# Cross-attention with a top-k mask and a mixture of experts on one core: the front of the work re-ordered over VectorE, ScalarE and GpSimd

## The chip, the core and the metric

The kernel runs on one core of one Trainium2 chip. The metric is the device time of one execution in microseconds (us). The kernel before takes 130.39 us (median of three runs, 130.18 to 130.52).

## What is computed

The input is four batches of 256 tokens with 256 features (x) and 256 context tokens with 64 features (ctx). Two stages follow each other, each with a residual:

```
# stage 1, per batch
Q = ctx @ Wq.T ; K = ctx @ Wk.T
sim = Q K^T / (sqrt(16) * 4)                     # 256 x 256
threshold = 76th largest of each row of sim      # int(0.3 * 256)
A = sigmoid(sim) * (sim >= threshold) ; A = (A + A^T) / 2
g = sigmoid(gamma_raw)
x1 = x + (1 - g) * layernorm(x) + g * A
# stage 2, all tokens
xn = layernorm(x1)
probs = softmax(xn @ gate_w) ; two best of 8 experts, their scores normalised, times alpha
h_e = gelu(xn @ fc1_w[e] + fc1_b[e]) ; y_e = h_e @ fc2_w[e] + fc2_b[e]
out = x1 + sum over e of combine[:, e] * y_e
```

## The kernel before

**Numbers.** The products of stage 2 are made in a reduced-precision 32-bit type, each operand split in a high and a low part, w = w_hi + w_lo, and three products are summed: hi*hi, hi*lo, lo*hi. So every expert's weights (128x1024 per partition layout, fc1 and fc2 together) need a high part (a cast, `weight_hi`) and a low part. For experts 0 and 1 GpSimd subtracts (`weight_lo(e, j)`, L675, j = 0 for fc1 and 1 for fc2). For experts 2 to 7 ScalarE writes -w_hi into w_lo (`weight_neg`, L559), and a DMA issued by GpSimd adds w to it in place (`weight_rest`, L671, below called the low-part DMA). PE waits for that DMA before `up(e)` of batch 0.

**Steps.** 32 steps s = 8b + e, batch b and expert e. On PE `up(s)` makes the hidden layer (12 products) and `down(s)` the output (12 products), down two steps behind up. Per step ScalarE does the gelu and the high part of the hidden layer (`hidden_hi`), GpSimd its low part (`hidden_lo`, h_lo, L698), and VectorE multiplies with the combine weight and adds (`add_expert`, acc, L1061). `up(s)` waits for the gelu of step s-2, `down(s)` for `add_expert(s-2)`.

**Batch b+1 beside the steps of batch b.** The mask and both layer norms of batch b+1 are spread over the steps of batch b. Batch 0 has no steps to hide behind: everything before `up(0)` is the front. What a front is, for batch 0, in the order of VectorE's program (L1073 to L1108): copy sim, mean and spread give a guess of the threshold; two sign counts on ScalarE (`signs_of`, `signs_again_of`) improve it (`middle_guess`, `better_guess`); `count_above` counts the values above the guess; `flag_few` and `flag_missed` flag rows for which the guess is too far off, PE sums the flags (`sum_missed`); `drop_above` removes the values above the guess, and two rounds of `take_eight`/`drop_eight` (MAX8 and MATCH_REPLACE8) find the 16 next; `choose` picks the threshold among them; `mask` multiplies; `add_masked` adds half of A to the base (x times mul1 plus add1, from `ln1_affine` and `base`). PE transposes the masked tile (`transpose_masked`, L374), VectorE's `residual` adds the transpose and makes the moments of the second layer norm, GpSimd its power -1/2 (`rstd`), VectorE `normalise` (xn, L971), PE transposes xn (`transpose_xn`), ScalarE and VectorE copy its high and low part (`xt_hi_of`, `xt_lo_of`), and `up(0)` starts.

**Order.** Each engine runs its own program in a hand-written order, and all waits are semaphores. On PE, after the similarities of the four batches (`similarities`, L357, with `sum_missed(0)` between those of batches 1 and 2), come `transpose_masked(0)`, 18 dummy products (`keep_warm(WARM_BEFORE_XN)`, L355), `transpose_xn(0)`, three more, then the steps. Loads are issued by the sync engine in one order (L307 to L317). On GpSimd the order is a list (L701 to L739), so a step that waits holds all behind it: there the high parts of experts 0 to 2, `rstd`, `base(0)`, the low parts, the low-part DMAs, and in the steps `hidden_lo`, `rstd`, the DMAs and `add_masked`. ScalarE has the high parts of experts 3 to 7 (L555).

## Time and profile before

| | |
|---|---|
| median of three runs | 130.39 us (130.18 to 130.52) |
| the profiled execution | 130.1 us, its span 128.3 us |
| PE busy | 119.2 us, 93% of the span |
| VectorE (DVE) busy | 96.2 us, 75% |
| ScalarE (ACT) busy | 87.6 us, 68% |
| GpSimd (POOL) busy | 65.0 us, 51% |
| read from HBM, written | 8.81 MB, 1.05 MB |

Engines in the rows: PE is TensorE, PEld its weight load, DVE VectorE, ACT ScalarE, POOL GpSimd, SP the sync engine. A row of the timeline has start, duration, engine, line, operation, out<-in, shapes, count, and in brackets the idle time before it with what ended it. Busy PE is not PE at its peak: the dummy products count as busy. Times are us from the start of the span.

### The profile page before, as it was taken

The numbers are of one execution on the slowest core, as the hardware profiler recorded it, in microseconds if no ns is written. First come the engines' busy times: TensorE is split into PE (matmuls) and PEld (weight loads), VectorE is DVE, ScalarE is ACT, GpSimd is POOL, SyncE is SP. The second block draws the span as 40 slices with busy tenths as digits, with TensorE's granted clock in tenths as the row PEclk, the third lists the DMA queues.
The fourth block names the chain that finished last, engine by engine and source line by source line (L and its number), as shares of the span: only waits on it lengthen the run. The fifth ranks groups of instructions, "written<-read, shape, count | busy, mean of one in ns | idle before, by whom it ended". The sixth has DMA issues, their size and how long they took to land.

```text
span 128.3 us, 2763 instructions
## 1 busy us (share of the span) xinstructions
PE 119.2 (93%) x904; PEld 108.6 (85%) x904; DVE 96.2 (75%) x399; ACT 87.6 (68%) x212; POOL 65.0 (51%) x66
## 2 busy tenths in 40 slices
PE   6796989899969999999999999999999999999990
PEld 3443656699949999999899999998999999999990
DVE  0068989886987898999979999999787337823481
ACT  3178999899999979454897784729646544555510
POOL 2039668638647944643097456512972545444400
PEclk9999999999999999999999999999999999999999
DMA  2999999952996000002000000200000002000002
GB/s 66 198 390 415 405 321 174 192 101 29 181 169 119 5 0 3 0 5 82 3 0 0 3 8 0 81 1 8 0 0 0 5 0 82 0 5 0 3 0 82
DMA packets 3380, 10.05 MB, mean 78 GB/s; under 512 B 396, under 2 KB 868, under 8 KB 3364
## 3 DMA queue, kind: packets, MB, share of 16 engines
q1 hardware_dynamic: 2500, 6.71, 14.7%
q0 software_dynamic: 864, 3.15, 14.3%
q8 instruction: 7, 0.11, 0.3%
q14 instruction: 9, 0.07, 0.2%
HBM read 8.81 MB, written 1.05 MB: 77 GB/s over the span
## 4 chain that ended last, share of the span: by engine, by line
PE 41%; DVE 36%; ACT 13%; issue 6%; POOL 1%; DVEq 0%; POOLq 0%; ACTq 0%
PE p_y L477 17%; PE p_h L455 16%; DVE acc L1061 8%; ACT h_act L579 3%; ACT w_lo L564 2%; ACT w_hi L557 2%; DVE top L886 2%; DVE above L842 2%; DVE stats L745 2%; ACT h_hi L587 2%; PE p_y L355 2%; DVE left L891 1%; DVE picked L1018 1%; ACT act_waste L543 1%; DVE best_f L1004 1%
## 5 line engine op out<-in xcount | busy, mean ns | idle before, releaser
L698 POOL TENSOR_TENSOR h_lo<-h_act,h_hi 128x512 fp32r<-128x512 f32 x31 | 40.2, 1300 | 45.4 <-ACT h_hi L587 32.6
L579 ACT ACTIVATE h_act<-p_h,small_sb 128x256 f32<-128x256 f32 x64 | 26.6, 467 | 19.4 <-PE p_h L455 19.3
L455 PE MATMUL p_h<-xt_hi,w_hi 128*128 128x256 f32 x128 | 32.9, 280 | 1.1 <-ACT h_act L579 1.0
L455 PE MATMUL p_h<-xt_hi,w_lo 128*128 128x256 f32 x128 | 32.6, 278 | 0.0
L1061 DVE SCALAR_TENSOR_TENSOR acc<-p_y,comb,acc 128x256 f32<-128x256 f32 x55 | 24.0, 475 | 11.0 <-PE p_y L477 10.2
L477 PE MATMUL p_y<-w_hi,h_hi 128*128 128x256 f32 x126 | 26.0, 288 | 1.0 <-DVE acc L1061 1.0
L455 PEld LDWEIGHTS p_h<-xt_hi,w_hi 128*128 128x128 f32 x128 | 24.1, 188 | 1.6 <-issue 1.5
L455 PE MATMUL p_h<-xt_lo,w_hi 128*128 128x256 f32 x128 | 25.3, 279 | 0.0
L477 PE MATMUL p_y<-w_lo,h_hi 128*128 128x256 f32 x126 | 24.9, 279 | 0.0
L477 PE MATMUL p_y<-w_hi,h_lo 128*128 128x256 f32 x126 | 24.9, 279 | 0.0
L455 PEld LDWEIGHTS p_h<-xt_hi,w_lo 128*128 128x128 f32 x128 | 24.1, 188 | 0.0
L587 ACT ACTIVATE h_hi<-h_act 128x512 fp32r<-128x512 f32 x32 | 20.2, 630 | 0.9
L477 PEld LDWEIGHTS p_y<-w_hi,h_hi 128*128 128x128 f32 x126 | 19.1, 189 | 1.7 <-issue 1.5
L455 PEld LDWEIGHTS p_h<-xt_lo,w_hi 128*128 128x128 f32 x128 | 19.5, 188 | 0.1
L477 PEld LDWEIGHTS p_y<-w_lo,h_hi 128*128 128x128 f32 x126 | 19.3, 189 | 0.0
L477 PEld LDWEIGHTS p_y<-w_hi,h_lo 128*128 128x128 f32 x126 | 19.2, 188 | 0.0
L355 PE MATMUL p_y<-warm 128*128 128x256 bf16 x30 | 6.5, 395 | 1.2 <-DVE warm L1073 1.2
L669 POOL CAST w_hi<-w_sb 128x1024 fp32r<-128x1024 f32 x3 | 3.1, 1035 | 7.0 <-DMA w_sb<-w 7.0
L886 DVE MAX8 top<-left 128x8 f32<-128x256 f32 x16 | 5.9, 410 | 0.8 <-DVE left L891 0.4
L355 PEld LDWEIGHTS p_y<-warm 128*128 128x128 bf16 x30 | 4.1, 140 | 2.8 <-DVE warm L1073 1.2
L564 ACT ACTIVATE w_lo<-w_hi 128x1024 fp32r<-128x1024 f32 x6 | 6.3, 1047 | 0.1
L593 ACT ACTIVATE x_sb<-x_sb,add,mul 128x256 f32<-128x256 f32 x6 | 3.3, 591 | 4.1 <-DVE add L791 4.1
(141 smaller groups left out, 191.1 us busy)
## 6 DMA issues: line engine op xcount, KB each, us to landing
w_sb<-w SPq DMA_DIRECT2D x8, 512.0 KB, 8.3
w_lo<-w POOLq DMA_DIRECT2D x6, 512.0 KB, 5.6
x_sb<-x SPq DMA_DIRECT2D x1, 768.0 KB, 8.5
out<-acc SPq DMA_DIRECT2D x3, 256.0 KB, 2.5
x_sb<-x SPq DMA_DIRECT2D x1, 256.0 KB, 4.4
out<-acc SPq DMA_DIRECT2D x2, 128.0 KB, 2.0
attn_sb<-attn SPq DMA_DIRECT2D x1, 192.0 KB, 5.1
small_sb<-small SPq DMA_DIRECT2D x1, 97.5 KB, 4.7
```

What stands on the lines that cost most here:

```text
L355: nc.tensor.matmul(p_y[1][:, 0:N], warm[:, 0:P], warm[:], start=True, stop=True)
L455: last = nc.tensor.matmul(dst, w_[:, e, 0, k, c * P:(c + 1) * P], v[:, b % 2, k, :], start=n == 0, stop=n == len(trio) - 1)
L477: last = nc.tensor.matmul(dst, v[:, s % (LAG + 1), k, t * P:(t + 1) * P], w_[:, e, 1, k, :], start=n == 0, stop=n == len(trio) - 1)
L557: nc.scalar.activation(w_hi[:, e], w_sb[:, e], ACT.Copy).then_inc(w_hi_ready, 1)
L564: nc.scalar.activation(w_lo[:, e], w_hi[:, e], ACT.Copy, scale=-1.0).then_inc(w_neg_ready, 1)
L579: last = nc.scalar.activation(h_act[:, s % 2, c], tiled(p_h[s % 2])[:, c, :], ACT.Gelu, bias=b1_sb[:, e, c:c + 1])
L587: nc.scalar.activation(h_hi[:, s % (LAG + 1)], h_act[:, s % 2], ACT.Copy).then_inc(h_hi_ready, 1)
L593: last = nc.scalar.activation(x_sb[:, b, t], x_sb[:, b, t], ACT.Identity, scale=mul1[:, b, t:t + 1], bias=add1[:, b, t:t + 1])
L669: nc.gpsimd.tensor_copy(w_hi[:, e], w_sb[:, e]).then_inc(w_hi_early, 1)
L698: nc.gpsimd.tensor_tensor(h_lo[:, s % (LAG + 1)], h_act[:, s % 2], h_hi[:, s % (LAG + 1)], ALU.subtract).then_inc(h_lo_ready, 1)
L886: step_of_tile(nc.vector.max(top[:, t, 8 * r:8 * r + 8], left[:, t]))
L1061: last = nc.vector.scalar_tensor_tensor(acc[:, b % 2, t], tiled(y_bank(s, t))[:, t, :], comb[:, b, t, 0, e:e + 1], so_far, ALU.mult, ALU.add)
```

## The change

- **Loads.** The small tensor (gamma, alpha, gate weights, biases, identity) is issued second instead of fourth.
- **Gamma.** ScalarE makes tanh of gamma, and the high part of the gate weights, right after its first copy; VectorE's `gamma_terms` stands at the very front instead of before `drop_above(0)`.
- **Batch 0's affine.** `ln1_affine(0)`, four instructions of 128x1, moves from VectorE to GpSimd.
- **Threshold of batch 0.** The two tiles' guess and count instructions are interleaved; `flag_few` and `flag_missed` become one instruction of 128x2 each instead of two of 128x1 (in every batch), and `flag_missed` stands after both tiles of `drop_above`.
- **Moments of batch 1.** `ln1(1)` moves on VectorE from between `add_masked(0)` and `residual(0)` to step 1, and GpSimd's `rstd` for it from step 0 to step 1.
- **Casts.** The high parts of experts 5, 6, 7 move from ScalarE to GpSimd (before step 0, in step 0 and in step 2); ScalarE keeps 3 and 4. GpSimd's list before the steps is re-ordered, and the low-part DMA of expert 4 moves from before step 0 into it, the DMAs of experts 5 to 7 one step back each.
- **ScalarE's order.** `sim_copy(1)` and `spread_of(1)` come before the negated weights of experts 2 and 3, `base(1)` one step later (step 3), the high part of b2 in step 5 instead of 3; VectorE's `b2_parts_of` in step 6 instead of 4.

PE's program keeps its order; only the count that `sum_missed` waits for changes.

```diff
--- before.py
+++ after.py
@@ -27,7 +27,9 @@
 REPLACED = -3.0e38
 ROUNDS = 2
 DAMPINGS = (0.8, 0.5)
-POOL_HI = 3
+POOL_HI = (0, 1, 2, 5, 6, 7)
+ACT_HI = (3, 4)
+POOL_HI_AT = {0: 6, 2: 7}
 WARM_FIRST = 9
 WARM_BEFORE_XN = 18
 B2_AFTER = 4
@@ -305,9 +307,9 @@
         def _(sp):
             first = 2 * D + N
             sp.dma_start(attn_sb[:, 0:first], attn[:, 0:first]).then_inc(attn_in, 16)
+            sp.dma_start(small_sb[:], small).then_inc(small_in, 16)
             sp.dma_start(x_sb[:, 0], x[:, 0:TILES]).then_inc(x_in[0], 16)
             sp.dma_start(attn_sb[:, first:], attn[:, first:]).then_inc(ctx_in, 16)
-            sp.dma_start(small_sb[:], small).then_inc(small_in, 16)
             sp.dma_start(w_sb[:, 0], w[:, 0]).then_inc(w_in[0], 16)
             for e in range(1, EXPERTS):
                 sp.dma_start(w_sb[:, e], w[:, e]).then_inc(w_in[e], 16)
@@ -341,7 +343,7 @@
 
             def sum_missed(b):
 
-                pe.wait_ge(missed_ready, (b + 1) * TILES)
+                pe.wait_ge(missed_ready, b + 1)
                 if b == 0:
                     pe.wait_ge(u_copied, 1)
                     pe.wait_ge(const_set, 2)
@@ -557,10 +559,10 @@
                 nc.scalar.activation(w_hi[:, e], w_sb[:, e], ACT.Copy).then_inc(w_hi_ready, 1)
 
             def weight_neg(e):
-                if e < POOL_HI:
-                    act.wait_ge(w_hi_early, e + 1)
+                if e in POOL_HI:
+                    act.wait_ge(w_hi_early, POOL_HI.index(e) + 1)
                 else:
-                    act.wait_ge(w_hi_ready, e - POOL_HI + 1)
+                    act.wait_ge(w_hi_ready, ACT_HI.index(e) + 1)
                 nc.scalar.activation(w_lo[:, e], w_hi[:, e], ACT.Copy, scale=-1.0).then_inc(w_neg_ready, 1)
 
             def xt_hi_of(b):
@@ -602,28 +604,27 @@
             act.wait_ge(m_ready, 1)
             nc.scalar.activation(m_sb[:], p_g[0:D, 0:D], ACT.Copy).then_inc(m_copied, 1)
             u_copy(0)
+            act.wait_ge(small_in, 16)
+            nc.scalar.activation(gam[:, 0:1], gamma_sb, ACT.Tanh, scale=0.5).then_inc(gam_th, 1)
+            nc.scalar.activation(gate_parts[:, :, 0], gate_sb, ACT.Copy).then_inc(gate_hi_ready, 1)
             sim_copy(0)
             spread_of(0)
             signs_of(0)
             signs_again_of(0)
-            act.wait_ge(small_in, 16)
-            nc.scalar.activation(gam[:, 0:1], gamma_sb, ACT.Tanh, scale=0.5).then_inc(gam_th, 1)
             for b in range(1, BATCHES):
                 u_copy(b)
             sigmoid(0)
+            weight_hi(3)
+            sim_copy(1)
+            spread_of(1)
             weight_neg(2)
-            weight_hi(3)
             weight_neg(3)
-            for b in range(1, BATCHES):
+            for b in range(2, BATCHES):
                 sim_copy(b)
-            nc.scalar.activation(gate_parts[:, :, 0], gate_sb, ACT.Copy).then_inc(gate_hi_ready, 1)
-            spread_of(1)
-            weight_hi(4)
-            weight_neg(4)
             signs_of(1)
             xt_hi_of(0)
             signs_again_of(1)
-            weight_hi(5)
+            weight_hi(4)
             for s in range(STEPS):
                 b, e = divmod(s, EXPERTS)
                 more = b + 1 < BATCHES
@@ -638,16 +639,19 @@
 
                     act.wait_ge(gap_ready, b + 1)
                     nc.scalar.activation(gap_th[:], gap[:], ACT.Tanh, scale=0.5).then_inc(gap_th_ready, 1)
-                if s < 3:
-                    weight_neg(5 + s)
                 if s < 2:
-                    weight_hi(6 + s)
-                if s == 3:
+                    weight_neg(4 + s)
+                if s in (1, 3):
+                    weight_neg(6 + s // 2)
+                if s == 5:
                     act.wait_ge(b2_in, 16)
                     nc.scalar.activation(b2_hi[:], b2_sb[:], ACT.Copy).then_inc(b2_hi_ready, 1)
                 if e == 2 and more:
                     sigmoid(b + 1)
-                    base(b + 1)
+                    if b:
+                        base(b + 1)
+                if s == 3:
+                    base(1)
                 if e == 5:
                     comb_hi_of(b)
                 if e == 4 and b + 2 < BATCHES:
@@ -685,6 +689,18 @@
                                                    add1[:, b, t:t + 1], ALU.mult, ALU.add)
                 last.then_inc(base_ready, 1)
 
+            def ln1_affine(b):
+
+                pool.wait_ge(gam_ready, 1)
+                pool.wait_ge(ln1_agg, (b + 1) * TILES)
+                pool.wait_ge(ln1_rstd, b + 1)
+                for t in range(TILES):
+                    nc.gpsimd.tensor_scalar(mul1[:, b, t:t + 1], rstd1[:, b, t:t + 1], gam[:, 2:3], ones[:], ALU.mult,
+                                            ALU.add)
+                    last = nc.gpsimd.tensor_scalar(add1[:, b, t:t + 1], mv1[:, b, t, 0:1], gam[:, 3:4],
+                                                   rstd1[:, b, t:t + 1], ALU.mult, ALU.mult)
+                last.then_inc(ln1_mul, 1)
+
             def add_masked(b):
 
                 pool.wait_ge(masked, (b + 1) * TILES)
@@ -706,30 +722,32 @@
             weight_hi(0)
             rstd(veps1, rstd1, 0, ln1_veps, ln1_rstd)
             weight_lo(0, 0)
-            weight_hi(1)
-            weight_hi(2)
+            ln1_affine(0)
             base(0)
-            weight_lo(1, 0)
-            weight_rest(2)
             pool.wait_ge(gate_hi_ready, 1)
             nc.gpsimd.tensor_tensor(gate_parts[:, :, 1], gate_sb, gate_parts[:, :, 0], ALU.subtract).then_inc(
                 gate_lo_ready, 1)
+            weight_hi(1)
+            weight_hi(2)
+            weight_lo(1, 0)
+            weight_rest(2)
+            rstd(veps2, rstd2, 0, ln2_veps, ln2_rstd)
+            pool.wait_ge(xn_ready, TILES)
+            weight_lo(0, 1)
             weight_rest(3)
-            pool.wait_ge(masked, TILES)
-            weight_lo(0, 1)
-            rstd(veps2, rstd2, 0, ln2_veps, ln2_rstd)
-            weight_rest(4)
-            pool.wait_ge(xn_ready, TILES)
             weight_lo(1, 1)
+            weight_hi(5)
             for s in range(STEPS):
                 b, e = divmod(s, EXPERTS)
                 more = b + 1 < BATCHES
                 if s < STEPS - 1:
                     hidden_lo(s)
-                if s == 0:
+                if s == 1:
                     rstd(veps1, rstd1, 1, ln1_veps, ln1_rstd)
-                if s < 3:
-                    weight_rest(5 + s)
+                if s < 4:
+                    weight_rest(4 + s)
+                if s in POOL_HI_AT:
+                    weight_hi(POOL_HI_AT[s])
                 if more and b and e == 0:
                     rstd(veps1, rstd1, b + 1, ln1_veps, ln1_rstd)
                 if more and e == 3:
@@ -827,16 +845,22 @@
                 nc.vector.tensor_scalar(neg_middle[:, b, t:t + 1], off_first[:, t:t + 1], -PER_COUNTS[0] / 2,
                                         neg_guess[:, b, t:t + 1], ALU.mult, ALU.add).then_inc(middle_ready, 1)
 
-            def better_guess(b, t):
+            def offset_again(b, t):
 
                 dve.wait_ge(signs_again_ready, b * TILES + t + 1)
                 nc.vector.tensor_scalar(off[:, t:t + 1], signs_again[:, b, t:t + 1], N - 2 * MIDDLE,
                                         spread[:, b, t:t + 1], ALU.add, ALU.mult).then_inc(off_ready, 1)
+
+            def second_guess(b, t):
                 dve.wait_ge(off_ready, b * TILES + t + 1)
                 nc.vector.tensor_scalar(guess[:, t:t + 1], off[:, t:t + 1], PER_COUNTS[1] / 2,
                                         neg_middle[:, b, t:t + 1], ALU.mult,
                                         ALU.subtract).then_inc(better_ready, 1)
 
+            def better_guess(b, t):
+                offset_again(b, t)
+                second_guess(b, t)
+
             def count_above(b, t):
                 dve.wait_ge(better_ready, b * TILES + t + 1)
                 nc.vector.tensor_scalar(above[:, t], sim[:, b, t], guess[:, t:t + 1], None, ALU.is_ge, ALU.add,
@@ -844,19 +868,16 @@
 
             def flag_few(b):
 
-                for t in range(TILES):
-                    dve.wait_ge(counted, b * TILES + t + 1)
-                    nc.vector.tensor_scalar(few[:, t:t + 1], count[:, t:t + 1], TOP_K - WINDOW, None,
-                                            ALU.is_lt).then_inc(few_ready, 1)
+                dve.wait_ge(counted, (b + 1) * TILES)
+                nc.vector.tensor_scalar(few[:], count[:], TOP_K - WINDOW, None, ALU.is_lt).then_inc(few_ready, 1)
 
             def flag_missed(b):
 
                 if b:
                     dve.wait_ge(missed_sum, b)
-                for t in range(TILES):
-                    dve.wait_ge(few_ready, b * TILES + t + 1)
-                    nc.vector.tensor_scalar(missed[:, t:t + 1], count[:, t:t + 1], TOP_K, few[:, t:t + 1],
-                                            ALU.is_ge, ALU.add).then_inc(missed_ready, 1)
+                dve.wait_ge(few_ready, b + 1)
+                nc.vector.scalar_tensor_tensor(missed[:], count[:], TOP_K, few[:], ALU.is_ge,
+                                               ALU.add).then_inc(missed_ready, 1)
 
             steps = [0]
 
@@ -876,9 +897,11 @@
                 for t in range(TILES):
                     dve.wait_ge(counted, b * TILES + t + 1)
                     if t == TILES - 1:
-                        flag_missed(b)
+                        if b == 0:
+                            flag_few(b)
                     step_of_tile(nc.vector.scalar_tensor_tensor(left[:, t], above[:, t], REPLACED, sim_of_tile(b, t),
                                                                 ALU.mult, ALU.add))
+                flag_missed(b)
 
             def take_eight(r):
                 for t in range(TILES):
@@ -1071,6 +1094,7 @@
 
 
             nc.vector.memset(warm[:], 1.0).then_inc(warm_set, 1)
+            gamma_terms()
             for t in range(1, TILES):
                 sim_copy(t)
             for t in range(TILES):
@@ -1084,13 +1108,13 @@
                 ln1_variance(0, t)
             for t in range(TILES):
                 middle_guess(0, t)
-            for t in range(TILES):
-                better_guess(0, t)
-                count_above(0, t)
-            flag_few(0)
-            gamma_terms()
+            offset_again(0, 0)
+            second_guess(0, 0)
+            offset_again(0, 1)
+            count_above(0, 0)
+            second_guess(0, 1)
+            count_above(0, 1)
             drop_above(0)
-            ln1_affine(0)
             take_eight(0)
             know_missed(0)
             drop_eight(0)
@@ -1099,7 +1123,6 @@
             choose(0)
             mask(0)
             add_masked(0)
-            ln1(1)
             residual(0)
             guesses(1)
             normalise(0)
@@ -1123,6 +1146,7 @@
                 if more and e == 1:
                     take_eight(0)
                 if s == 1:
+                    ln1(1)
                     combine(0)
                 if more and e == 1:
                     drop_eight(0)
@@ -1137,7 +1161,7 @@
                     take_eight(1)
                     choose(nxt)
                     mask(nxt)
-                if s == 4:
+                if s == 6:
                     b2_parts_of()
                 if more and e == 5:
                     residual(nxt)
```

## Rows read from the trace of the kernel before

**Rows 1.** The page: busy time and instructions of the engines.

```profile
PE 119.2 (93%) x904; PEld 108.6 (85%) x904; DVE 96.2 (75%) x399; ACT 87.6 (68%) x212; POOL 65.0 (51%) x66
```

**Rows 2.** The chain that ended last, in order of time: start, us, what.

```profile
18.93 0.66 DVE stats L745 x2
...
19.92 0.75 DVE x L957 x2
...
22.57 0.43 DVE xn L971
...
38.60 1.60 PE p_h L455 x12
```

**Rows 3.** The timeline of PE in the front.

```profile
15.57 1.91 PE L339 MATMUL p_y<-attn_sb,u_sb 64*128 64x256 f32 x4
18.02 1.08 PE L379 MATMUL p_a<-small_sb,half 128*128 128x128 f32 x4 [0.54 <-DVE half L941]
18.90 3.89 PE L355 MATMUL p_y<-warm 128*128 128x256 bf16 x18
23.14 0.31 PE L391 MATMUL p_x<-small_sb,xn 128*128 128x128 f32 x1 [0.35 <-DVE xn L971]
```

**Rows 4.** Who waited for whom: PE, from 24 to 64 us (total, times, longest).

```profile
PE p_h L455 <- ACT h_act L579: 1.0, 1, 1.0
```

**Rows 5.** The timeline of VectorE in the front.

```profile
13.77 0.21 DVE L789 TENSOR_SCALAR mul<-rstd,gam 128x1 f32<-128x1 f32 x1
14.38 0.74 DVE L886 MAX8 top<-left 128x8 f32<-128x256 f32 x2
17.06 0.22 DVE L897 SCALAR_TENSOR_TENSOR chosen<-small_sb,count,top 128x16 f32<-128x16 f32 x1
17.39 0.48 DVE L941 SCALAR_TENSOR_TENSOR half<-p_s,threshold,half 128x256 f32<-128x256 f32 x1
```

**Rows 6.** The timeline of GpSimd up to 28 us.

```profile
0.75 0.10 POOL L702 MEMSET ones<- 128x1 f32 x1
9.62 0.70 POOL L665 TENSOR_TENSOR rstd<-veps,neg_half 128x2 f32<-128x2 f32 x1
11.49 2.02 POOL L669 CAST w_hi<-w_sb 128x1024 fp32r<-128x1024 f32 x2
14.57 1.09 POOL L684 TENSOR_SCALAR x_sb<-x_sb,mul,add 128x256 f32<-128x256 f32 x2 [1.07 <-DVE add L791]
15.64 1.27 POOL L677 TENSOR_TENSOR w_lo<-w_sb,w_hi 128x512 fp32r<-128x512 f32 x1
19.10 0.21 POOL L715 TENSOR_TENSOR gate_parts<-small_sb,gate_parts 128x16 fp32r<-128x16 f32 x1 [1.24 <-ACT gate_parts L619]
```

**Rows 7.** The timeline of VectorE and GpSimd, where they work at once.

```profile
39.22 1.28 POOL L698 TENSOR_TENSOR h_lo<-h_act,h_hi 128x512 fp32r<-128x512 f32 x1 [2.56 <-ACT h_hi L587]
39.46 1.31 DVE L1040 SCALAR_TENSOR_TENSOR b_parts<-b_hi,small_sb,b_sb 24x256 fp32r<-24x256 f32 x1 [0.59 <-ACT b_hi L647]
45.90 0.46 DVE L1033 SCALAR_TENSOR_TENSOR comb_parts<-comb_hi,small_sb,p_g 24x256 fp32r<-24x256 f32 x1
...
82.53 1.29 POOL L698 TENSOR_TENSOR h_lo<-h_act,h_hi 128x512 fp32r<-128x512 f32 x1 [1.44 <-ACT h_hi L587]
82.83 1.02 DVE L1004 CAST best_f<-best_at 128x4 f32<-128x4 uint32 x1
```

**Rows 8.** ScalarE's timeline from the first xt_hi copy to step 0's high part.

```profile
23.73 0.38 ACT L571 ACTIVATE xt_hi<-p_x 128x256 fp32r<-128x256 f32 x1 [0.55 <-PE p_x L391]
27.18 0.61 ACT L587 ACTIVATE h_hi<-h_act 128x512 fp32r<-128x512 f32 x1
```

**Rows 9.** DMA issues by line: KB each, median us from issue to landing.

```profile
small_sb<-small SPq DMA_DIRECT2D x1, 97.5 KB, 4.7
```

**Rows 10.** The low-part DMAs' line on GpSimd: durations of issue, spread of landing.

```profile
L673 POOL DMA_DIRECT2D w_lo<-w x6: 869/880/1002, 16.9 to 35.8; - x6
DMA to landing us min/median/max: 5.4/5.6/5.9
```

## The prediction

> **What bounds the kernel now.** I began with the page: PE is busy 93% of the span, but dummy products count as busy [rows 1], so the question is where PE's real work could start earlier or waits. The chain that ended last, read in order of time, is VectorE's in the front: moments of batch 1 at 18.93, `residual` at 19.92, xn at 22.57 [rows 2]. Next PE's timeline: the last similarities end at 17.48, the masked tiles are turned from 18.02 to 19.10, the 18 dummies run from 18.90 to 22.79, and xn is turned at 23.14 after an idle 0.35 us that VectorE's xn ended [rows 3]. Everything up to 23.14 is front, and what it loses there comes straight off the end if the steps keep their pace. In the steps up to 64 us PE's longest wait is 1.0 us for a gelu [rows 4], ahead of up(5) at 38.60 [rows 2]: a shift of the front also needs batch 0's steps to be fed earlier, not only started earlier. A measurement of this kernel tells a difference from none at about 0.3% (130.0 to 130.8 us).
>
> **VectorE's front.** Three gamma instructions and four of the affine leave; the affine took 0.61 us (13.77 to 14.38), and a gamma instruction is of the same kind and no longer [rows 5]. With the interleaved guesses and the merged flags I put MAX8 some 1.1 us earlier, at 13.2 to 13.5. Unhindered, `choose` (17.06) and `mask` (17.39) would be at 16.1 and 16.5 [rows 5]. Behind the mask `ln1(1)` goes, 0.99 us (18.93 to 19.92) [rows 2], so `residual` follows as soon as the masked tiles are turned.
>
> **What is late next: GpSimd in VectorE's way.** Beside GpSimd's h_lo from 39.22 to 40.50 VectorE's b_parts, reading two tensors of the on-chip memory, took 1.31 us and ended 0.27 after it; comb_parts, the same operation with one input from PE's banks, took 0.46. The cast best_f took 1.02 us and ended at 83.85, when GpSimd's operation ended (83.82) [rows 7]. So such an instruction stands still until the GpSimd operation that runs ends. Before, `choose` (two inputs, above_sb and top) fell at 17.06 behind GpSimd's last subtraction, 15.64 to 16.91 [rows 5, 6]; after, GpSimd has no pause there. From 11.49, when `weight_lo(0, 0)` is done, it has the affine, base(0) 1.10, the gate's low part 0.2, two casts 2.02 and `weight_lo(1, 0)` 1.25 [rows 6]. No row shows the affine on GpSimd: four instructions of 128x1, between four memsets at 0.10 (0.4 us) and four of the power instruction at 0.66 (2.6 us). I take 0.7, nearest to the 128x16 subtraction of 0.21 [rows 6]. Then `weight_lo(1, 0)` runs from about 15.5 to 16.7, `choose` waits 0.6 us until 16.7, and the mask starts at 17.0 instead of 17.39: -0.4 us. The new two-column flags may be held too, by base(0); `choose` waits anyway, so that costs nothing.
>
> By the Trainium skill, SBUF — State Buffer, section "Who interferes with whom", a VectorE instruction with two inputs in SBUF is blocked by any GpSimd instruction that reads SBUF, so by the casts as well. The rows above show it for two-input GpSimd work only; the rule adds a case to the rivals and nothing to the sum.
>
> **From mask to up(0).** Before, mask 17.39, dummies 18.90: 1.51 us between. After: dummies from 18.5, PE's similarities (end near 17.3) being done [rows 3]. The 18 dummies take 3.89 us, now to 22.4. `residual` starts near 18.7 and xn comes 2.65 later (19.92 to 22.57 before), 21.4 plus 0.4 for the instruction [rows 2]: ready ahead of the dummies, so PE, not VectorE, now sets the turn of xn, at 22.35 against 23.14: **-0.8 us**, and the idle 0.35 goes. The power instruction for it finds GpSimd free: the low-part DMA ahead of it waits for ScalarE's second negated weight until about 16.85 and issues in 1.0. The early tanh of gamma costs nothing: ScalarE idles there for PE's first similarity, and the small load, issued about 1.1 us earlier, lands by 6.0 even if it takes its old 4.7 us [rows 9].
>
> **Are the steps fed 0.8 us earlier?** ScalarE loses three casts of 1 us and has slack. GpSimd gets them. xt_hi's copy starts at 22.93, and from there to the end of step 0's h_hi it is 4.06 us as before (23.73 to 27.79), one cast between the two then and now [rows 8]: 27.0. GpSimd then: hidden_lo(0) 1.25, DMA of expert 4 0.88, cast 1.01, hidden_lo(1) 1.25, power 0.66 [rows 6, 7, 10], and issues expert 5's low-part DMA at 32.1. It lands 5.6 us later (5.4 to 5.9) [rows 10], and `up(5)` starts at 37.85; before it started at 38.60 [rows 2], after the 1.0 us wait for the gelu [rows 4]. So the gelu's wait becomes a DMA's wait, and the shift at up(5) is -0.75. Expert 4's lands at 33.8, where up(4) would be at 33.2: 0.6 us of wait, swallowed by the next. Expert 6 and 7 have over 1 us. ln1(1), 1.0 us in step 1, fills VectorE's wait for the tanh of the gap; b2_parts in step 6 meets slack of about 1 us before batch 1's xn. After up(5) the order is the old one, all shifted. `base(1)`, a step later, waits for GpSimd's cast of expert 7 on ScalarE's queue: ready near 38.5, its gelu behind it at 39.3, needed by PE at 41.3.
> One more rule: DMA: Bandwidth & Descriptors, section "Anatomy of one DMA", of the Trainium skill has such a transfer at 2.0 us plus its bytes over 436 GB/s, an estimate of 3.2 us for 512 KB, by which up(5) would wait for nothing. The trace's 5.4 to 5.9 us disagrees and decides.
>
> **Sum.** -0.8 at the turn of xn, -0.75 at up(5), and two fewer flag instructions per batch where VectorE's chain holds PE in batches 1 and 2: 0.1 us each. Together -1.0: 130.1 becomes 129.1 in the profiled execution (span 127.3). The median of before stands 0.3 above its profiled execution: **129.4 us**.
>
> **The rivals.**
> - *No hold at choose.* GpSimd's affine is as short as memsets, or the hold does not fall there. Then the mask is at 16.5, the similarities' end (17.3) and the dummies set the turn of xn near 21.75, -1.4, and up(5) follows at -1.4: 128.8 us, with -0.1 more 128.7. For it: ends of 0.4 us are near. Against: a continuous GpSimd queue.
> - *The front barely moves.* The affine costs GpSimd 2.6 us: the casts end at 17.4, and if casts hold VectorE (the skill's rule), `choose` waits for that, the mask is at 17.7 and the dummies end at 23.1: about zero, less 0.2 from the flags: 130.2 us. Or VectorE is held at several places (flags, add_masked).
> - *Slower: the low-part DMA of expert 5.* It stands behind the power instruction, which waits for ln1(1), behind best_f and MAX8 of step 1. ln1(1) ends near 30.3, the queue asks for it at 31.45, and up(5) is where it was before when the power starts at 32.2. If best_f is held by 1.0 us [rows 7] and GpSimd's queue runs 1 us late besides, with a landing of 5.9, up(5) is at 39.2: +0.6, 131.0 us. It decides from 0.75 us of lateness on.
> - *The change doesn't do what it says*: VectorE's front is freed, but the 18 dummies are kept in PE's order. This is in the sum already, as the limit of 3.89 us after the turn of the masked tiles.
>
> **Chances.** Forecast, holding 128.9 to 129.9: 0.46. No hold: 0.28. Barely moves: 0.17. Slower: 0.09. Range: 128.3 (no hold, and a landing of 5.4) to 130.4, which leaves out most of the slower case. Faster by over 0.3%: 0.46 + 0.28 + 0.05 of the third = 0.79; same 0.13; slower 0.08.
>
> **What would show it.** `choose` starts before 16.7 and lasts 0.6 us instead of 0.22, ending with `weight_lo(1, 0)`; mask 17.0. PE turns xn with no idle time named for xn, at 22.35. PE waits for DMA before up(4) and up(5), and up(5) starts near 37.85. From up(6) on all rows are the old ones shifted by 0.75 to 1.0. Wrong it is if `choose` lasts 0.22, if the turn of xn waits for VectorE, if up(5) starts without a DMA's wait or after 38.6, or if the shift at up(5) is lost by the end.

## The result, and the profile after

The changed kernel takes **138.74 us** (median of 4, 138.27 to 139.53) against 130.37 us before, a ratio of 1.065 [1.059, 1.071]: 8.4 us slower, where 1 us faster was forecast. The profiled execution is the slowest of the four: 139.53 us, span 137.7.

The page of the changed kernel: its span, busy times as in [rows 1], and the clock's row in 40 slices.

```profile
span 137.7 us, 2755 instructions
PE 122.5 (89%) x904; PEld 112.4 (82%) x904; DVE 105.3 (76%) x387; ACT 85.1 (62%) x209; POOL 69.5 (50%) x73
PEclk9999999996995599999999999999999999999999
```

VectorE, with 12 instructions fewer, is busy 9.1 us longer: its instructions last longer. The timeline of VectorE in the changed kernel says which, those of the front first (start, us; compare [rows 5]):

```profile
13.37 0.74 DVE L909 MAX8 top<-left 128x8 f32<-128x256 f32 x2
16.05 0.47 DVE L920 SCALAR_TENSOR_TENSOR chosen<-small_sb,count,top 128x16 f32<-128x16 f32 x1
16.45 1.30 DVE L920 SCALAR_TENSOR_TENSOR chosen<-small_sb,count,top 128x16 f32<-128x16 f32 x1
17.68 0.47 DVE L964 SCALAR_TENSOR_TENSOR half<-p_s,threshold,half 128x256 f32<-128x256 f32 x1
...
26.21 1.16 DVE L872 TENSOR_SCALAR few<-count 128x2 f32<-128x2 f32 x1
27.29 1.85 DVE L902 SCALAR_TENSOR_TENSOR left<-above,sim 128x256 f32<-128x256 f32 x2
29.06 2.92 DVE L879 SCALAR_TENSOR_TENSOR missed<-count,few 128x2 f32<-128x2 f32 x1
...
36.33 4.74 DVE L1046 TENSOR_TENSOR comb<-weight,small_sb 128x48 f32<-128x48 f32 x1
```

MAX8 came 1.0 us earlier, as meant. But the first `choose` lasted 0.47 and the second 1.30 us instead of 0.22 and 0.23, and behind it the mask was 0.3 us **later** than before. In the steps, a 128x2 flag lasted 2.92 us and the 128x48 product comb 4.74; the same comb takes 0.21 elsewhere. GpSimd's timeline at the same time:

```profile
14.48 2.02 POOL L673 CAST w_hi<-w_sb 128x1024 fp32r<-128x1024 f32 x2
16.46 1.25 POOL L681 TENSOR_TENSOR w_lo<-w_sb,w_hi 128x512 fp32r<-128x512 f32 x1
...
22.91 1.28 POOL L681 TENSOR_TENSOR w_lo<-w_sb,w_hi 128x512 fp32r<-128x512 f32 x1 [0.85 <-DVE xn L994]
24.13 0.89 POOL L677 DMA_DIRECT2D w_lo<-w  x1
24.77 1.60 POOL L681 TENSOR_TENSOR w_lo<-w_sb,w_hi 128x512 fp32r<-128x512 f32 x1
26.02 1.32 POOL L673 CAST w_hi<-w_sb 128x1024 fp32r<-128x1024 f32 x1
27.40 1.45 POOL L714 TENSOR_TENSOR h_lo<-h_act,h_hi 128x512 fp32r<-128x512 f32 x1
28.80 0.89 POOL L677 DMA_DIRECT2D w_lo<-w  x1
29.39 1.34 POOL L673 CAST w_hi<-w_sb 128x1024 fp32r<-128x1024 f32 x1
30.39 1.56 POOL L714 TENSOR_TENSOR h_lo<-h_act,h_hi 128x512 fp32r<-128x512 f32 x1
34.99 0.72 POOL L669 TENSOR_TENSOR rstd<-veps,neg_half 128x2 f32<-128x2 f32 x1 [3.04 <-DVE veps L775]
35.67 0.90 POOL L677 DMA_DIRECT2D w_lo<-w  x1
36.33 1.55 POOL L714 TENSOR_TENSOR h_lo<-h_act,h_hi 128x512 fp32r<-128x512 f32 x1
37.57 1.15 POOL L677 DMA_DIRECT2D w_lo<-w  x1
38.16 1.61 POOL L673 CAST w_hi<-w_sb 128x1024 fp32r<-128x1024 f32 x1
39.17 1.82 POOL L714 TENSOR_TENSOR h_lo<-h_act,h_hi 128x512 fp32r<-128x512 f32 x1
```

But for 0.06 us at 27.34, no idle time stands between the rows from 22.91 to 31.95, and none from 34.99 to 40.99. Two single VectorE instructions stood still across several GpSimd operations: the flag missed(1), 29.06 to 31.98, across the rest of a DMA issue, a cast and an h_lo, and comb, 36.33 to 41.07, across h_lo, a DMA issue, a cast and h_lo. Each ended when the run did. Others got their turn inside a run: the first `choose` ended at 16.52, with the cast (16.50), although `weight_lo(1, 0)` followed at once (16.46); few(1) ended at 27.37 with a cast (27.34); and the second `left` (1.51 of the 1.85 us are its own) ended at 29.14, when h_lo had ended (28.85) and GpSimd was issuing a DMA. PE's waits, of the whole span, say what the holds cost:

```profile
PE p_y L479 <- DVE acc L1084: 4.7, 3, 4.2
PE p_a L352 <- DVE missed L879: 2.8, 1, 2.8
```

`sum_missed(1)` stands in PE's order ahead of `down(0)`, so PE stood from 29.3 to 32.03 for the flag; `down(2)` needs `add_expert(0)`, which VectorE had behind comb. After each wait the granted clock was halved. Stretches of the changed kernel (busy PE, PEld, DVE, ACT, POOL, then PEclk, the DMA share and GB/s), and the chain:

```profile
29.00:32.00 3.00, 0.28 (x3) 0.07 (x1) 3.00 (x3) 0.63 (x1) 2.95 (x3) 0.95 0.58 75
32.00:35.00 3.00, 2.97 (x15) 2.93 (x16) 2.90 (x21) 2.25 (x4) 0.01 (x1) 0.50 0.55 107
39.00:43.50 4.50, 0.39 (x4) 0.19 (x2) 4.46 (x13) 1.88 (x4) 2.87 (x3) 0.82 1.06 199
43.50:49.00 5.50, 5.43 (x26) 5.42 (x27) 3.38 (x12) 2.61 (x9) 2.51 (x2) 0.52 0.47 83
```

```profile
36.33 4.75 DVE comb L1046
...
43.57 2.90 PE p_y L479 x12
46.47 2.49 PE p_h L457 x12
```

PE idles, then works at 0.50, the 1.2 GHz level. The sum to up(5)'s end: waits 2.8 + 4.2; down(0) 2.7 us (32.15 to 34.88) and down(2) 2.90 where a down takes 1.39 in the kernel before, up(5) 2.49 for 1.60: 3.7 more; minus 0.5 us that the front did gain, minus 1.4 for two waits of before that vanish (gelu 1.0 [rows 4], acc 0.4). That is 8.8 of the 9.4 us between the spans; the rest lies where the clock still rises.

### The profile page after: what moved, and what is told of

It is laid out like the page before. It is cut to its first block, busy times and chain, and to the rows that moved or that the text cites. A ratio compares the mean times of both kernels' runs of the same rounds, so it can differ in the third digit from the quotient of the medians.

```text
span 137.7 us, 2755 instructions
## 1 busy us (share of the span) xinstructions
PE 122.5 (89%) x904; PEld 112.4 (82%) x904; DVE 105.3 (76%) x387; ACT 85.1 (62%) x209; POOL 69.5 (50%) x73
## 3 DMA queue, kind: packets, MB, share of 16 engines
HBM read 8.81 MB, written 1.05 MB: 72 GB/s over the span
## 4 chain that ended last, share of the span: by engine, by line
PE 44%; DVE 34%; POOL 7%; issue 5%; DMA 4%; ACT 2%; SPq 1%; DVEq 1%; POOLq 0%; ACTq 0%
PE p_y L479 21%; PE p_h L457 18%; DVE acc L1084 6%; DMA w_sb<-w 4%; DVE comb L1046 4%; DVE missed L879 2%; POOL w_hi L673 2%; DVE picked L1041 2%; DVE few L872 2%; DVE left L902 2%; DVE best_f L1027 2%; DVE above L866 2%; DVE left L914 1%; DVE stats L763 1%; DVE top L909 1%
## 5 line engine op out<-in xcount | busy, mean ns | idle before, releaser
L714 POOL TENSOR_TENSOR h_lo<-h_act,h_hi 128x512 fp32r<-128x512 f32 x31 | 41.3, 1333 | 42.3 <-ACT h_hi L589 28.8
L479 PE MATMUL p_y<-w_hi,h_hi 128*128 128x256 f32 x126 | 27.1, 298 | 4.7 <-DVE acc L1084 4.7
L479 PE MATMUL p_y<-w_hi,h_lo 128*128 128x256 f32 x126 | 25.9, 288 | 0.0
L479 PE MATMUL p_y<-w_lo,h_hi 128*128 128x256 f32 x126 | 25.9, 288 | 0.0
L479 PEld LDWEIGHTS p_y<-w_hi,h_hi 128*128 128x128 f32 x126 | 20.0, 197 | 5.5 <-issue 5.3
L479 PEld LDWEIGHTS p_y<-w_lo,h_hi 128*128 128x128 f32 x126 | 20.3, 198 | 0.0
L479 PEld LDWEIGHTS p_y<-w_hi,h_lo 128*128 128x128 f32 x126 | 20.2, 197 | 0.0
L673 POOL CAST w_hi<-w_sb 128x1024 fp32r<-128x1024 f32 x6 | 7.3, 1227 | 7.4 <-DMA w_sb<-w 7.4
L669 POOL TENSOR_TENSOR rstd<-veps,neg_half 128x2 f32<-128x2 f32 x8 | 6.1, 766 | 5.5 <-DVE veps L775 3.0
L980 DVE TENSOR_TENSOR x<-x_sb,p_a 128x256 f32<-128x256 f32 x8 | 3.1, 419 | 4.3 <-PE p_a L381 2.5
```

The lines of the kernel that those rows point to most:

```text
L479: last = nc.tensor.matmul(dst, v[:, s % (LAG + 1), k, t * P:(t + 1) * P], w_[:, e, 1, k, :], start=n == 0, stop=n == len(trio) - 1)
L669: nc.gpsimd.tensor_tensor(rs[:, b, :], veps[:, b, :], neg_half[:], ALU.pow).then_inc(ready, 1)
L673: nc.gpsimd.tensor_copy(w_hi[:, e], w_sb[:, e]).then_inc(w_hi_early, 1)
L714: nc.gpsimd.tensor_tensor(h_lo[:, s % (LAG + 1)], h_act[:, s % 2], h_hi[:, s % (LAG + 1)], ALU.subtract).then_inc(h_lo_ready, 1)
```

## The experiments

Theory A, formed from the two traces: a VectorE instruction that needs what GpSimd uses gets no turn until GpSimd's queue pauses; the change made the queue unbroken. Rivals: the casts alone cost it (ScalarE or DMA order); the merged flags alone cost it; the clock costs it. Before p3 ran, a rival D was on record too: a waiting instruction gets its turn at the end of each GpSimd operation, and the next one is held anew. The kernel before, timed beside each run, took 130.44 to 130.53 us.

**x1: casts of experts 5 to 7 and their DMAs as before, the rest changed.**

```
-POOL_HI = (0, 1, 2, 5, 6, 7)    ACT_HI = (3, 4)             POOL_HI_AT = {0: 6, 2: 7}
+POOL_HI = (0, 1, 2)             ACT_HI = (3, 4, 5, 6, 7)    POOL_HI_AT = {}
```

> The changed kernel with the casts of experts 5, 6, 7 on ScalarE and the low-part DMAs where they were before; all else of the change stays. Theory A (VectorE's two-input and paired-port instructions starve while GpSimd works without a pause, and the moved casts took the pauses away): no VectorE instruction in batch 0's steps is held over 1.3 us, PE's waits of 2.8 and 4.2 us go, the clock stays at its upper level, 129.3 to 130.2 us. Rival B (the merged two-column flags are what is held, whoever casts): few and missed are still held by over 1 us, 132 us or more. Rival C (the re-ordered front itself, DMA or the small load): over 133 us.

130.68 us, 1.002 [1.001, 1.003]. So the three casts, with the places of their low-part DMAs, are 8.1 of the 8.4 us. The time is still 0.5 us above what theory A had expected. The front's gain stayed lost: the second `choose` still lasted 1.31 us, held by `weight_lo(1, 0)`, and few(1) took 1.08, the two `left` 1.85.

**x2: flags one column at a time, as before, the rest changed.**

> The changed kernel with the flags as two one-column instructions again (missed still behind both drops). Theory A: few and missed take 0.2 us each, but left in batch 0's step 0 and comb in step 1 are still held, comb until GpSimd's queue pauses (3 us or more); 133 to 138 us. Rival B: 129.5 to 130.5 us.

137.99 us, 1.061 [1.055, 1.066]. PE's wait for missed is gone, but the hold went to the next instructions. VectorE's timeline in x2:

```profile
26.34 2.78 DVE L905 SCALAR_TENSOR_TENSOR left<-above,sim 128x256 f32<-128x256 f32 x2
29.04 0.32 DVE L882 TENSOR_SCALAR missed<-count,few 128x1 f32<-128x1 f32 x2
30.42 1.59 DVE L1030 CAST best_f<-best_at 128x4 f32<-128x4 uint32 x1
34.02 2.93 DVE L1044 TENSOR_SCALAR picked<-small_sb,best_f,score 128x8 f32<-128x8 f32 x4
36.99 2.85 DVE L1047 TENSOR_TENSOR weight<-picked 128x16 f32<-128x16 f32 x1
```

The flags of one column are not held: the two few take 0.27 us at 26.15, beside GpSimd's subtraction and cast, and the two missed 0.32, beside its DMA issue. PE waited 6.6 us once for acc instead of 2.8 + 4.2. Merging the flags chose the place of the hold, not its cost. Rows with x2 or x4 add several instructions up; instruction by instruction the longest `picked` here is a single hold of 2.35 us, ended by h_lo's end (36.69), and the weight row is one instruction of 2.85.

**x3: the kernel before with only the casts and their DMAs moved to GpSimd.**

> The kernel before with nothing but the casts of experts 5, 6, 7 and the low-part DMAs moved as in the change. Theory A: one-column flags are not held, but left and one of picked, weight, comb are, 1.5 to 5 us; 132 to 137 us. Rival B: within 0.5% of the kernel before, 129.8 to 131.0 us. Rival C: the same as B.

130.95 us, 1.005 [1.003, 1.006]. The casts alone cost 0.5 us. That is the rivals' number: theory A had expected 132 to 137 us. One `picked` is held for 2.32 us (30.71 to 33.03, across a cast and an h_lo), but GpSimd's queue keeps a pause of 2.25 us ahead of the first h_lo, since `weight_lo(1, 0)` and `(0, 1)` lie in the front. PE waited 0.6 us in all for acc (1.0 in the kernel before), and 1.7 us for a low-part DMA ahead of an up. So the casts by themselves are nearly harmless, and so is the rest (x1); only together do they cost 8 us. That this is because they close the pauses is argued from the rows, not shown by x3.

**x4: the changed kernel, with two waits that make GpSimd yield.**

```
+ if s == 0: pool.wait_ge(missed_ready, 2)     # ahead of the cast of expert 6
+ if s == 2: pool.wait_ge(comb_ready, 1)       # ahead of the DMA and cast of step 2
```

> The changed kernel with two waits more on GpSimd: it lets VectorE's missed of batch 1 go before the cast of expert 6, and comb of batch 0 before the low-part DMA of expert 6 and the cast of 7. Nothing of GpSimd's work leaves. Theory A: missed and comb end with the one GpSimd instruction that runs when they come, under 1.6 us each instead of 2.9 and 4.7; PE's 4.2 us wait falls below 1.5 us; 129.5 to 132.5 us. If it is the number of casts and not their closeness: 136 us or more.

135.31 us, 1.037 [1.033, 1.040]: 3.4 of the 8.4 us back, fewer than expected: a miss. missed(1) now took 1.25, comb 0.21, but best_f (2.10) and one of the `picked` (2.12) were held and PE waited 3.7 us for acc. To yield at two places shifted the hold to the next places.

**x5: x1 with `weight_lo(0, 1)` put into GpSimd's idle time of the front.**

> The run with the casts back on ScalarE, and besides GpSimd's low part of expert 0's second half before the power instruction (where GpSimd idled from 18.8 to 21.1) instead of behind xn. Theory A: GpSimd has a pause again between its last low part and h_lo(0), so few and the two left of batch 1 are no longer held (1.08 and 1.85 us there), and the 0.7 us that the front gained reaches the end: 129.3 to 130.1 us. If the holds in step 0 were hidden anyway: 130.7 us, no change against that run.

131.77 us, 1.009 [1.006, 1.011], a miss. What it aimed at happened: left(1) took 0.76 instead of 1.85 us. But the subtraction met `add_masked`. VectorE's row, then GpSimd's:

```profile
18.74 2.44 DVE L974 TENSOR_TENSOR x_sb<-x_sb,half 128x256 f32<-128x256 f32 x2
...
18.96 1.59 POOL L683 TENSOR_TENSOR w_lo<-w_sb,w_hi 128x512 fp32r<-128x512 f32 x1
```

The pair lasted 2.44 us (0.75 before), the first of them 2.10 across the rest of a DMA issue and the whole subtraction. PE waited 2.0 us for xn, and the clock was 0.59 from 24 to 28 us.

**x6: the changed kernel with 12 dummy products ahead of `sum_missed(1)` and 18 ahead of `down(2)`.**

> The changed kernel with 12 dummy products on PE ahead of sum_missed(1) and 18 ahead of down(2), in a bank free at that time: the waits stay, the engine is busy in them. It measures what of the loss is clock: down(0), down(2) and up(5) took about 4 us more than at the upper level. If the clock's fall is a loss of its own: the granted clock stays at its upper level, 134.3 to 136.0 us. If VectorE's holds set the end anyway: 137.5 us or more.

139.22 us, 1.068 [1.065, 1.072]. The clock was 1.0 up to 44 us, and nothing was gained, but the holds fell elsewhere (best_f 3.04, one `picked` 2.35, weight 2.87), PE waited 4.0 us for acc, and the clock was 0.57 from 44 to 48. The second branch of the expectation is met. The run does not separate the clock; with the clock kept up over the first wait the end came no earlier, as it would if VectorE set it.

**p1 and p3: the kernel before with one cast, or three in a row, on GpSimd at step 10.** They write a scratch tensor that nobody reads.

```
+ if s == 10:
+     pool.wait_ge(gating, 24)
+     for n in range(1):                        # p3: range(3)
+         nc.gpsimd.tensor_copy(probe[:, n], w_sb[:, 0])
```

> The kernel before with one cast more on GpSimd (128x1024, 1.03 us, into a tensor nobody reads), started when the scores of batch 1's combine are nearly done (59.1 us), where GpSimd is otherwise idle until 63.9. Both theories: the picked or weight instruction of VectorE that comes meanwhile takes about 1.0 us more than its 0.29 or 0.18. It is the measure for the next run.

> The same with three casts back to back. Theory A (a held VectorE instruction gets no turn between GpSimd instructions that follow each other without a pause): one instruction is held by about 3.0 us, until the third cast ends. Rival D (it gets its turn at each boundary, as the prediction took it): the first is held by 1.0 us, and each later one anew by up to 1.0, so no single instruction takes over 1.4 us.

131.19 and 134.37 us, one execution each. The timeline at the probe, GpSimd and VectorE, of p1 and then of p3, each with the shortest, middle and longest of the four `picked` in ns:

```profile
59.28 1.04 POOL L733 CAST probe<-w_sb 128x1024 fp32r<-128x1024 f32 x1 [0.40 <-DVE score L1019]
...
59.31 1.61 DVE L1023 TENSOR_SCALAR picked<-small_sb,best_f,score 128x8 f32<-128x8 f32 x4
...
L1023 DVE TENSOR_SCALAR picked<-small_sb,best_f,score x4: 280/281/1029, 59.3 to 60.6; 128x8 f32<-128x8 f32 x4
```

```profile
59.34 3.02 POOL L733 CAST probe<-w_sb 128x1024 fp32r<-128x1024 f32 x3 [0.40 <-DVE score L1019]
...
59.38 3.20 DVE L1023 TENSOR_SCALAR picked<-small_sb,best_f,score 128x8 f32<-128x8 f32 x4
...
L1023 DVE TENSOR_SCALAR picked<-small_sb,best_f,score x4: 279/1054/1078, 59.4 to 62.3; 128x8 f32<-128x8 f32 x4
```

Without a probe the four `picked` take 0.87 us. One cast: 0.74 more; three in a row: 2.33 more, and they end at 62.58, after the third cast (62.36). It would be easy to take the 3.20 us for one long hold. The third line of each view says otherwise: in p1 one `picked` took 1.03 us and the others 0.28; in p3 three took 1.03 to 1.08 us, one per cast, and the last 0.28. They start at 59.38, 60.32, 61.31 and 62.30, the casts at 59.34, 60.33 and 61.31. So at the end of each cast the waiting instruction got its turn, and the next was held by the next cast. **p3 speaks for rival D and against theory A**, which had expected a single hold of about 3.0 us.

What, then, lets one instruction stand across several operations, as missed(1) and comb did? The kept traces of all runs fall into two kinds, read by GpSimd's starts. (1) The next operation's row starts 0.03 to 0.06 us before the end of the one ahead: here every held VectorE instruction went at that end (the casts of p3, the first `choose`, and b_parts in the kernel before, below). (2) The next row starts 0.24 to 0.63 us before that end: here single instructions stood across it (among them missed(1), comb, best_f in x2, x4, x6 and x7, `picked` in x3, weight in x2, x6 and x7), although at four such ends, each with a DMA issue next, a `picked` got its turn. Each case of the second kind has an issue of a low-part DMA ahead of it or at it in the same run of GpSimd's queue; none of the first kind has one ahead of it. So the rows tie the long holds to a DMA issue followed by work without a pause, and a pause, even the 0.06 us at 27.34, brings back the first kind. No run varied the DMA issue alone, so this is not shown as the cause.

The two runs also price the clock: p1's 0.74 us on VectorE made PE wait 1.0 us, without a fall of the clock, and cost 0.7 us; p3 made it wait 2.6:

```profile
60.00:64.00 4.00, 2.14 (x19) 1.94 (x18) 3.90 (x12) 0.15 (x1) 2.36 (x3) 1.00 0.00 0
64.00:68.00 4.00, 3.26 (x18) 3.29 (x19) 3.58 (x13) 3.94 (x9) 1.59 (x2) 0.70 0.01 2
68.00:72.00 4.00, 4.00 (x34) 3.97 (x32) 2.50 (x13) 2.44 (x8) 3.44 (x3) 0.88 0.00 2
```

p3 cost 3.8 us: 2.3 of hold, and about 1.5 that the clock's fall accounts for ((1 - 0.70) x 4 + (1 - 0.88) x 4 = 1.7).

**x7: the changed kernel, `weight_lo(0, 1)` issued when base(0) is summed.**

> The changed kernel with GpSimd's first low part issued as soon as base(0) is summed, in the gap that GpSimd's timeline shows from 18.98 to 21.34 us, instead of behind xn; the casts of experts 5 to 7 stay on GpSimd. It takes one operation of 1.2 to 1.6 us and one DMA issue out of the unbroken stretch of 22.91 to 31.95 us, so that stretch ends at 29.5 to 30.5. Theory A (a VectorE instruction with two SBUF inputs gets no turn until GpSimd pauses): missed(1) is held to 29.5 to 30.5 at most instead of 31.98 and TensorE's wait for it falls from 2.8 us to 1 or less; the second stretch of 35 to 41 us moves earlier with it but stays unbroken, so one instruction of 2.5 us or more remains there. Time 133 to 136. The low part now runs beside the residual additions, which may be held by up to 1.6 us. Rival (TensorE's order alone or the moved front is at fault, the length of GpSimd's stretch is not): within 0.5 us of 138.7.

138.09 us, 1.058 [1.055, 1.062]: a miss, near the rival's 138.7 though 0.1 us outside its 0.5. missed(1) was free, but best_f was held for 3.07 us (28.77 to 31.84), behind a DMA issue and across a cast that ended at 30.54 and an h_lo that ended at 31.80. One `picked` took 2.34 and weight 2.86 us, and PE waited 6.3 us for acc. One operation less left the second run unbroken.

**x8: the kernel before with only the flags merged.**

> The kernel before with only the two flags of a batch merged into one instruction of two columns each. Theory A: such an instruction is held by GpSimd, where one column is not, but GpSimd has pauses in the kernel before, so each hold lasts one GpSimd operation at most, 1.6 us, and mostly falls while few(1) and missed(1) stand ahead of nothing urgent: 130.0 to 131.2 us. Rival (the merged form is what costs the changed kernel its time by itself): over 132 us.

131.19 us, 1.006 [1.004, 1.008]. The merged few(0) took 1.04 us, 12.50 to 13.54, beside the casts of experts 1 and 2 that end at 13.5; in the kernel before, two flags of one column at 12.37, beside the same casts, take 0.27. That hold by a single operation is as large as the loss (0.75 us). So a cast does hold VectorE here, and only in the merged form.

**v1: the changed front with GpSimd's pauses kept.** Casts as in x1, flags as in x2, and:

```
             weight_hi(2)
+            pool.wait_ge(base_sum, 1)
             weight_lo(1, 0)
...
-            weight_lo(1, 1)
...
                     hidden_lo(s)
+                if s == 0:
+                    weight_lo(1, 1)
```

> A version that keeps the changed front and gives GpSimd its pauses back: casts of experts 5 to 7 on ScalarE as before, flags one column at a time as before, weight_lo(1,0) only after base(0) is summed, weight_lo(1,1) only after h_lo(0). Theory A: the choice of tile 3 is held by the cast of expert 2 alone and ends by 16.7 us instead of 17.7, the mask runs by 17.0, the xn turn on TensorE starts by 22.2 instead of 23.1, where 18 dummies end it; few and left of batch 1 stay at 0.1 to 0.6 us. Time 128.9 to 129.8, under the kernel before by 0.5 to 1.4 us. Rival (the front's gain is not TensorE's, or the holds of batch 1 fall elsewhere): 130.2 to 131.0, with a held VectorE instruction of over 1.5 us between 24 and 38 us.

**129.26 us**, 0.991 [0.989, 0.994]: faster than both kernels and within the expectation of theory A. Rival D fits it as well: the longest hold before 45 us is best_f's, 1.09 us, by one operation. VectorE's and PE's front in v1 ([rows 5], [rows 3] before):

```profile
16.53 0.23 DVE L927 SCALAR_TENSOR_TENSOR chosen<-small_sb,count,top 128x16 f32<-128x16 f32 x1
16.71 0.48 DVE L971 SCALAR_TENSOR_TENSOR half<-p_s,threshold,half 128x256 f32<-128x256 f32 x1
```

```profile
18.31 4.04 PE L357 MATMUL p_y<-warm 128*128 128x256 bf16 x18
22.15 0.38 PE L393 MATMUL p_x<-small_sb,xn 128*128 128x128 f32 x1
```

The mask is 0.7 us earlier, xn's turn 1.0 us. up(0) starts 0.8 us earlier (23.50 for 24.26) and up(5) 1.6 (37.01 for 38.60 [rows 2]), as the gelu's wait of 1.0 us [rows 4] is gone too. At batch 1's xn 0.8 us is left (44.41 for 45.25), and the same at the end of the span. Where the rest goes between up(5) and that xn wasn't tried.

**v2: v1 with 14 dummies.**

> v1_pauses_kept with 14 dummy matmuls ahead of the xn transposes instead of 18. If TensorE's dummies are what ends last at the xn turn there, it starts up to 0.8 us earlier and the time falls by 0.3 to 0.6 us against v1_pauses_kept, the granted clock staying at 1.0 up to 30 us. If xn itself is what ends last, the time is that of v1_pauses_kept within 0.2 us.

129.18 us, 0.990 [0.987, 0.993], the time of v1. xn's turn came 0.4 us earlier (21.73), then waiting 0.3 us for xn, and up(0) 0.3; the 0.3 are not in the time. The first branch of the expectation falls, the second holds.

## Why the prediction was wrong

The step that failed is **"ScalarE loses three casts of 1 us and has slack. GpSimd gets them"**. I followed GpSimd's queue only for when its own results were due, and asked at `choose` alone who would be held by it. What the casts and the moved DMA issues do to VectorE in batch 0's steps, and through it to PE, stood in the sum at nothing; x1 puts it at 8.1 us.

With it failed the size of a hold, **"So such an instruction stands still until the GpSimd operation that runs ends"**, where a DMA issue stands in an unbroken run: missed(1) stood 2.92 and comb 4.74 us, across two and three operations that compute. Elsewhere the rule holds: in p3 (1.03 to 1.08 us, a cast each), at both `choose`, and already in the kernel before, where b_parts of [rows 7] ended at 40.77, soon after h_lo's end (40.50), while GpSimd went straight on:

```profile
40.47 1.46 POOL L692 TENSOR_TENSOR x_sb<-x_sb,half 128x512 f32<-128x512 f32 x1
```

The other half of that reading was weaker than it looked: comb_parts (45.90) started ahead of GpSimd's operation (46.06), so its 0.46 us does not show that an input from PE's banks escapes a hold. `left` of batch 0 does, which reads PE's bank beside the casts of experts 1 and 2 and takes its usual time:

```profile
12.86 0.42 DVE L880 SCALAR_TENSOR_TENSOR left<-above,p_s 128x256 f32<-128x256 f32 x1
```

By its other steps:
- *MAX8 1.1 us earlier, at 13.2 to 13.5*: right, 13.37.
- *The affine on GpSimd 0.7 us*: mis-sized. It took 1.3 (four of 0.34, from 11.84 to 13.13). The casts therefore ended at 16.5 instead of 15.5 and `weight_lo(1, 0)` at 17.7 instead of 16.7.
- *`choose` waits 0.6 us, mask 17.0*: the mechanism was right, the size not: the first was held 0.2 by the cast, the second 1.1 by `weight_lo(1, 0)`, mask 17.68. v1, which takes the subtraction away from there, has it at 16.71.
- *The casts hold too*: I cited this rule as adding nothing to the sum. The Trainium skill, SBUF — State Buffer, "Who interferes with whom", was right: `choose`, with two inputs, was held by a cast, for 0.2 us here and for 0.7 in x5 (0.92 us, both ended with the cast). x8's few(0), p1 and p3 are holds by casts too, of a form that the rule as cited does not name. For VectorE's two-port modes the same section gives the shared ports to whoever issues first, for the whole instruction. The turns in p3 agree with that. By that alone best_f in x7 would have gone at the cast's end, 30.54; it ended at 31.84, and the run decides.
- *A flag held by base(0) costs nothing*: true of batch 0 (0.17 and 0.15 us, not held). For batch 1 the same flag stands ahead of `sum_missed(1)` on PE, 2.8 us.
- *Turn of xn at 22.35 with the dummies as the limit*: 22.65, limited by xn, which the late mask delayed. -0.5 instead of -0.8. The 18 dummies took 3.23 us, and from 3.02 to 4.05 in the traces of all runs: the 3.89 of one trace was no fixed limit.
- *Expert 5's low-part DMA decides up(5)*: PE waited for no low part. up(5) started at 46.27, 7.7 us late.
- *The rivals*: the slower one had the wrong mechanism and 131.0 us. "Held at several places (flags, add_masked)" named the right one, but as a case of 130.2 us; neither the number of held instructions nor a hold across several operations was priced.

What stays open: what makes a hold run on behind a DMA issue; a run like p3 with a DMA issue ahead of its casts would test it and wasn't tried. Then the share of the clock in the 8.4 us. The rows put it at 3.7 us and p3 supports such a price, but x6, meant to separate it, moved the holds. Which form of access makes picked (128x8, its scalars read from memory) one of the held, a row doesn't show. And missed(0) of the changed kernel, 128x2 with two inputs, ran in 0.15 us at 13.30 beside base(0) (13.22 to 14.34) where both theories have it held; GpSimd's starts may be too rough to tell, and it wasn't tried.

## What to carry to other kernels

Before moving work to GpSimd, list the VectorE instructions beside it that have two inputs in on-chip memory or write several columns of a copy or scalar form. Price each at up to one GpSimd operation (1.0 to 1.3 us here), and look for a DMA issue in GpSimd's queue with work right behind it: there a single VectorE instruction stood for up to 4.7 us. GpSimd's share of busy time over the span (50% here, 51% before) says nothing of it. v1 shows a way out: fewer operations in a row and pauses between them. Put GpSimd work where VectorE reads PE's banks or waits; merging two one-column instructions into one of two columns can make it one of those that wait. A PE instruction that only gathers flags doesn't belong ahead of PE's real work when its source can be held.

And before reading a long row as one hold, ask whether it is one instruction: a row with x4 can be four short holds.

## What the runs showed that I had not expected

- Casts back to back give a waiting VectorE instruction its turn at each boundary (p3: 1.03 to 1.08 us, one per cast). Behind a DMA issue one instruction stood across several operations: 2.92 us (missed), 3.07 (best_f in x7), 4.74 (comb, across h_lo, a DMA issue, a cast and h_lo).
- GpSimd hardly pays. Its rows of 1.32 to 1.61 us for a cast that takes 1.01 alone, and of 1.55 to 1.82 for h_lo, begin before the operation ahead has ended; from end to end the casts at 29.39 and 38.16 took 1.05 us each and the h_lo behind them 1.22. Of these only h_lo at 27.40, with `left` just ahead of it, took longer from end to end, 1.45 for 1.29. (GpSimd's spans are rough.)
- One column isn't held (0.27 for two beside casts), two columns are (1.04).
- A 128x1 scalar operation takes GpSimd 0.34 us, more than the 128x16 subtraction's 0.21.
- PE's wait of 1.0 us left the clock at 1.0; after waits of 2.0 (x5), 2.6 (p3), 2.8 and 4.2 us rows show a granted clock of 0.50 to 0.70.
